# A token-embedding, gated-scan and ternary feed-forward kernel: the low-rank branch moved into row and column tiles of the matmul array

## What is computed

```
h = take(embed_table, x)                                   # [64, 256, 256]
h = h + minGRU(layernorm(h))     # f = sigmoid(x Wf'), i = sigmoid(x Wi'), g(x Wh')
                                 # state[t] = f*state[t-1] + i*g, started at 0.5
h = h + ffn(layernorm(h)):
    a = bitlinear(x, w_fc) + gate * (x @ v.T @ fast_b.T @ u.T)   # 256 -> 1024, and rank 16
    r = maximum(a, 0)
    return bitlinear(r * r, w_proj)                               # 1024 -> 256
```

## Time and profile before

| | before |
|---|---|
| median of 3 runs | 933.69 us (933.27 to 934.51) |
| time of the profiled execution | 933.25 us |
| its span, first to last instruction | 931.4 us |
| around the span (933.25 - 931.4) | 1.85 us |
| mean granted TensorE clock | 0.992 |
| busy: PE, DVE, ACT, POOL | 96%, 80%, 84%, 50% |

### The profile page before, as it was taken

How to read it: one execution, slowest core, us unless ns; L and a number is a source line. 1 busy time by engine, 2 the same in 40 slices (tenths; PEclk the granted TensorE clock), 3 DMA queues, 4 the chain that set the end, 5 groups by cost and what they waited for, 6 DMA issues and landing times.

```text
span 931.4 us, 17427 instructions
## 1 busy us (share of the span) xinstructions
PE 893.2 (96%) x5169; PEld 511.4 (55%) x5169; DVE 745.0 (80%) x1309; ACT 781.3 (84%) x1159; POOL 462.6 (50%) x457
## 2 busy tenths in 40 slices
PE   3889999999999999999999999999999999999976
PEld 2335555555555555555555555655555555555544
DVE  6799888878888878888887788888888888877663
ACT  4578998888898888889888889988888998888765
POOL 6545554556655455664545566554556555522110
PEclk9989999999999999999999999999999999999989
DMA  4223344342333333233333323323332332343220
GB/s 143 46 50 62 94 67 91 97 91 61 82 83 78 85 96 87 58 87 79 78 90 95 79 65 85 81 73 96 96 74 69 84 83 73 96 91 70 64 71 24
DMA packets 229579, 73.91 MB, mean 79 GB/s; under 512 B 204342, under 2 KB 224384, under 8 KB 229552
## 3 DMA queue, kind: packets, MB, share of 16 engines
q1 hardware_dynamic: 223408, 69.38, 31.3%
q0 software_dynamic: 6144, 4.21, 2.0%
HBM read 27.68 MB, written 24.64 MB: 56 GB/s over the span
## 4 chain that ended last, share of the span: by engine, by line
PE 91%; ACT 3%; DVE 2%; issue 2%; POOL 1%; DMA 1%; SPq 0%; ACTq 0%; POOLq 0%; DVEq 0%
PE bank L762 35%; PE y_ps L719 23%; PE bank L801 23%; PE bank L805 6%; PE bank L702 3%; PE turned L730 2%; ACT normed L476 1%; ACT relu L528 1%; ACT sq L541 1%; DMA w_raw<-wh 0%; POOL rows_raw L379 0%; DMA x_cols<-x_rows 0%; DVE stats L877 0%; POOL rstd L394 0%; DVE y_sb L1064 0%
## 5 line engine op out<-in xcount | busy, mean ns | idle before, releaser
L801 PE MATMUL bank<-x_cols,fc_t 128*128 128x512 f16 x1024 | 265.4, 382 | 0.0
L389 POOL TENSOR_SCALAR var_eps<-moments 128x4 f32<-128x4 f32 x64 | 59.7, 933 | 355.1 <-DVE moments L881 355.0
L762 PE MATMUL bank<-x_cols,w_hi 128*128 128x512 f16 x768 | 229.8, 381 | 4.6 <-ACT cand_lin L517 3.0
L762 PE MATMUL bank<-x_cols,w_lo 128*128 128x512 f16 x768 | 229.4, 380 | 0.0
L719 PE MATMUL y_ps<-proj_t,sq_hi 128*128 128x256 bf16 x1024 | 225.6, 273 | 2.1 <-DVE sq_lo L1056 2.0
L719 PE MATMUL y_ps<-proj_t,sq_lo 128*128 128x256 bf16 x1024 | 225.6, 273 | 0.0
L379 POOL DMA_INDIRECT rows_raw<-table,idx_now x128 | 161.3, 1260 | 60.2 <-issue 31.0
L528 ACT ACTIVATE relu<-bank,relu_scale 128x512 f32<-128x512 f32 x256 | 165.2, 688 | 13.0 <-PE bank L805 13.0
L801 PEld LDWEIGHTS bank<-x_cols,fc_t 128*128 128x128 bf16 x1024 | 100.9, 99 | 115.4 <-issue 3.2
L1056 DVE TENSOR_TENSOR sq_lo<-sq,sq_hi 128x1024 f16<-128x1024 f32 x128 | 150.4, 1214 | 15.0 <-ACT sq L541 15.0
L476 ACT ACTIVATE normed<-h,shift,rstd 128x256 f32<-128x256 f32 x256 | 132.9, 605 | 8.7 <-POOL shift L397 8.7
(11 more groups left out here) (129 smaller groups left out, 929.0 us busy)
## 6 DMA issues: line engine op xcount, KB each, us to landing
out<-out_sb SPq DMA_DIRECT2D x32, 512.0 KB, 2.9
spill<-hid_blocks SPq DMA_DIRECT2D x30, 256.0 KB
hid_rows<-spill SPq DMA_DIRECT2D x120, 64.0 KB
rows_raw<-table,idx_now POOLq DMA_INDIRECT x128, 2.8
x_cols<-x_rows SPq DMA_TRANSPOSE x124
sq<-w_fc SPq DMA_DIRECT2D x1, 1024.0 KB
pj_raw<-w_proj SPq DMA_DIRECT2D x1, 1024.0 KB
w_raw<-wf SPq DMA_DIRECT2D x1, 256.0 KB
```

The costliest lines, as they stand in the source:

```text
L762: ins = pe.matmul(bank[gate_bank[p]][:, :], w[:, k, q, :], x_part(0, par, part)[:, :, k, :], start=(k == 0 and w is w_hi and part == 0), s ...
L801: pe.matmul(dst[:, :], fc_t[:, f, k, :], x_part(1, 0, part)[:, :, k, :], start=(k == 0 and part == 0), stop=False)
```

## The change

The low-rank branch is done in other shapes, and the PSUM banks are given out by another rule. Line numbers in this section with an a (L730a) are of the changed kernel.

- `low_a` shrinks to 32 columns. `low_parts` (L730a) issues four matmuls of 32 output rows, one for each combination of input half and input part, into four column tiles of the array: rows 0-31, 32-63, 64-95 and 96-127 of `low_ps`, half of the PSUM tensor `turned`. They are four partial sums, not yet added.
- ScalarE copies them to float16 (`part_high`), VectorE takes the remainder (`part_low`), and `low_sums` (L740a, L741a) multiplies both by `spread`, a 0/1 matrix made at the start, which adds the partial sums and repeats the result over all 128 rows.
- ScalarE (`low_high`) and VectorE (`low_low`) split that result again, into `low_hi` and `low_lo`.
- `narrow` (L836a) replaces the eight matmuls L805 by sixteen that use 32 rows each: for four hidden blocks at a time, block i uses rows 32i to 32i+31, so four row tiles of the array, first with `low_hi`, then with `low_lo`.
- In a steady step blocks 0 and 1 are opened by `wide`, then `narrow(0, 2)` runs over blocks 0 to 3, which ends blocks 0 and 1 and opens 2 and 3, and `wide` ends those; then blocks 4 to 7 in the same way. `free(f)` is the wait for the block's bank.
- Bank of gate p: `(p + 2*par) % 4`; bank of block f: `(f + 2 + 2*par) % 4`.
- The four transposes of the scanned state go to the other half of `turned` (`turn_upper`).

```diff
-                for k in range(KD):
-                    for part in range(2):
-                        ins = pe.matmul(bank[0][:, :], low_a[:, k, :], x_part(1, 0, part)[:, :, k, :],
-                                        start=(k == 0 and part == 0), stop=(k == KD - 1 and part == 1))
-                ins.then_inc(low_done, 1)
+                for k in range(KD):
+                    for part in range(2):
+                        at = slice(BLOCK * (2 * k + part), BLOCK * (2 * k + part + 1))
+                        ins = pe.matmul(low_ps[at, :], low_a[:, k, :, :].rearrange("p a r -> p (a r)"),
+                                        x_part(1, 0, part)[:, :, k, :], start=True, stop=True)
+                ins.then_inc(part_done, 1)
+
+            def low_sums(m):
...
+                pe.wait_ge(part_hi_ready, m + 1)
+                pe.wait_ge(part_lo_ready, m + 1)
+                pe.matmul(low_ps, spread[:, :], part_hi[:, :], start=True, stop=False)
+                pe.matmul(low_ps, spread[:, :], part_lo[:, :], start=False, stop=True).then_inc(low_done, 1)
...
+                def free(f):
+
+                    if f > 3:
+                        pe.wait_ge(relu_ready, FC * m + f - 3)
...
+                def narrow(first_f, opened):
+
+                    for f in range(first_f + opened, first_f + 4):
+                        free(f)
+                    for part, ready in ((low_hi, low_hi_ready), (low_lo, low_lo_ready)):
+                        pe.wait_ge(ready, m + 1)
+                        for i in range(4):
+                            f, at = first_f + i, slice(BLOCK * i, BLOCK * (i + 1))
+                            ins = pe.matmul(fc_bank(f, par)[:, :], low_u[at, f * P:(f + 1) * P], part[at, :],
+                                            start=(part is low_hi and i >= opened),
+                                            stop=(part is low_lo and i < opened))
+                            if part is low_lo and i < opened:
+                                ins.then_inc(fc_done, 1)
...
+                    for p in range(3):
+                        gate(p)
...
+                        project(n - 2)
+                    gate(3)
+                    if steady:
+                        low_parts(n, m)
+                    gate(4)
+                    gate(5)
...
+                    if steady:
+                        low_sums(m)
...
+                wide(0, True)
+                wide(1, True)
+                if steady and front:
+                    narrow(0, 2)
+                    wide(2, False)
+                    wide(3, False)
+                else:
+                    low_sums(m)
+                    wide(2, True)
+                    wide(3, True)
+                    narrow(0, 4)
+                wide(4, True)
+                wide(5, True)
+                if front and not first:
+                    turn_upper(n)
+                narrow(4, 2)
+                wide(6, False)
...
+                wide(7, False)
```

On ScalarE and VectorE:

```diff
+            def part_high(m):
+
+                act.wait_ge(part_done, m + 1)
+                wait(act, low_done, m)
+                act.activation(part_hi[:, :], low_ps, ACT.Copy).then_inc(part_hi_ready, 1)
...
-                act.activation(low[:, :], bank[0][:, :], ACT.Copy).then_inc(low_hi_ready, 1)
+                act.activation(low_hi[:, :], low_ps, ACT.Copy).then_inc(low_hi_ready, 1)
...
+                part_high(m)
+                if front:
+                    evict(n, par, 1, 1, inp, ACT.Sigmoid)
+                    evict(n, par, 1, 2, cand_sig, ACT.Sigmoid)
+                    evict(n, par, 1, 3, cand_lin, ACT.Identity, 0.5)
                 low_high(m)
-                if front:
-                    evict(n, 1, 2, cand_sig, ACT.Sigmoid)
-                    evict(n, 1, 3, cand_lin, ACT.Identity, 0.5)
                 back(n)
...
-                low_half()
+                part_low()
                 if ahead:
                     x_low(0, n + 1)
                 if front:
                     candidate(1)
+                low_low()
+                if front:
                     weigh(1)
                     scan(1)
```

More of the change, by code:

```diff
@@ L97, in build @@
         hid_rows = sb("hid_rows", [P, TILES, P])
-        low = sb("low", [P, CHUNK], F16)
+        part_hi = sb("part_hi", [P, CHUNK], F16)
+        part_lo = sb("part_lo", [P, CHUNK], F16)
+        low_hi = sb("low_hi", [P, CHUNK], F16)
+        low_lo = sb("low_lo", [P, CHUNK], F16)
         relu = sb("relu", [P, FC // 2, 2, CHUNK])
@@ L598, in step @@
                     scale_fc(1)
-                    evict(1, 1, 2, cand_sig, ACT.Sigmoid)
-                    evict(1, 1, 3, cand_lin, ACT.Identity, 0.5)
+                    part_high(0)
+                    evict(1, par, 1, 2, cand_sig, ACT.Sigmoid)
+                    evict(1, par, 1, 3, cand_lin, ACT.Identity, 0.5)
                     low_high(0)
@@ L741, in step, with gate @@
                 steady = not isinstance(n, int) or n > 2
-                n_late = second or steady
+                def gate(p):
+                    e, g = divmod(p, 3)
+                    if p < 4:
+                        wait(pe, relu_ready, FC * (n - 2) + 5 + p)
+                        if first:
+                            pe.wait_ge(gate_taken, 8)
+                    else:
+                        pe.wait_ge(gate_taken, 8 * n + (4, 4 if start else 3)[p - 4])
+                    q = 2 * g + e
+                    for k in range(KD):
+                        for w in (w_hi, w_lo):
+                            for part in range(2):
+                                ins = pe.matmul(gate_bank(p, par)[:, :], w[:, k, q, :], x_part(0, par, part)[:, :, k, :],
+                                                start=(k == 0 and w is w_hi and part == 0),
+                                                stop=(k == KD - 1 and w is w_lo and part == 1))
+                    ins.then_inc(gate_done, 1)
@@ new lines, in free, with wide @@
+                def free(f):
+                    if f > 3:
+                        pe.wait_ge(relu_ready, FC * m + f - 3)
+                    elif front:
+                        pe.wait_ge(gate_taken, 8 * n + (2, 5, 6, 8)[f])
+                    else:
+                        pe.wait_ge(relu_ready, FC * (n - 2) + (7, 8, 5, 6)[f])
+                def wide(f, opens):
+                    if opens:
+                        free(f)
+                    if first:
+                        pe.wait_ge(fc_landed[f // 4], 16)
+                    for k in range(KD):
+                        for part in range(2):
+                            ins = pe.matmul(fc_bank(f, par)[:, :], fc_t[:, f, k, :], x_part(1, 0, part)[:, :, k, :],
+                                            start=(opens and k == 0 and part == 0),
+                                            stop=(not opens and k == KD - 1 and part == 1))
+                    if not opens:
+                        ins.then_inc(fc_done, 1)
@@ L1139, in residual, with part_low, low_low @@
                     measure(1, c, h1[:, at, :, :])
-                def low_half():
+                def part_low():
+                    dve.wait_ge(part_hi_ready, m + 1)
+                    wait(dve, low_done, m)
+                    dve.tensor_tensor(part_lo[:, :], low_ps, part_hi[:, :], ALU.subtract).then_inc(part_lo_ready, 1)
+                def low_low():
                     dve.wait_ge(low_hi_ready, m + 1)
-                    dve.tensor_tensor(low[64:P, :], bank[0][64:P, :], low[64:P, :], ALU.subtract)\
-                        .then_inc(low_ready, 1)
+                    wait(dve, fc_done, FC * m)
+                    dve.tensor_tensor(low_lo[:, :], low_ps, low_hi[:, :], ALU.subtract).then_inc(low_lo_ready, 1)
                 if start:
```

195 lines of the change are left out of this document (87 added, 108 removed).

## The result

The changed kernel takes **981.87 us** (median of 4 executions, 981.03 to 982.74). The kernel before, run beside it on the same chip, takes 933.61 us. The ratio is 1.0515, with a 95% interval of 1.0497 to 1.0534: slower by 48 us. The forecast was 966.0 in a range of 946 to 992: the sign and the mechanism came out, and a third of the loss (15.9 of 48.3 us) was missing.

What follows compares the result with a forecast made beforehand. PE was taken to bound the kernel, never waiting in a steady step. From 933.25 us, 29 steady steps of +0.90 (0.30 + 0.35 + 0.25) add 26.1, start and end 6.6: 966.0 us, range 946 to 992.

Steps and rivals of the forecast that it cites:

- PE's own work: Matmul slots and projection on PE: 7 slots added, 12 removed, so the step would shrink by 1.08 to 26.20 us.
- The wait for `low_lo`: After gate 5, PE waits some 0.5 us for DVE's `low_lo`, done 2.87 us after that gate's end.
- The wait for relu 3: Before `narrow(4, 2)`, PE waits another 0.9 us for ACT; relu 0 to relu 3's end takes 4.46.
- Distance s between tiles: Time between starts of neighbouring tiles: 0 to 0.098 us, middle 0.05 taken, 0.35 a step.
- Change of shape d: Switching between array shapes, three times a step: 0 to 0.163 us each, middle 0.08 taken, 0.25 in all.
- Transposed inputs: Needed 1.73 us earlier, before gate 4; landing 2.81 after issue, 16.15 against PE's 16.06 to 16.3: nearly limiting, costing nothing.
- the ring: Chain from one `narrow(4, 2)` to the next that sets a steady step: 27.58 against 27.28, +0.30 us before tile costs.
- a first wait for DMA `x_cols` longer than both others: Sign against the prediction: PE's wait for transposed inputs exceeding its waits for `low_lo` and for the relu.
- Start and end: Steps 1, 2 and the last lose 1.9, about 2 and 2.7 us, together 6.6.
- Serial tiles: Rival: tiles don't go side by side, each tiled matmul takes a slot; 2.6 us a step, total 1015 us; chance 0.12.
- "Faster": Rival: both waits total under 1.08 us, so PE never waits for relu 3; step 26.20, total 900 us; chance 0.05.

Runs made afterwards that it cites:

- kernel 4: Column tiles after gate 4, four relus ahead of two squares, and low copies first, all three against the changed kernel: 936.02 us, a step of 27.05.
- Experiment 2: Against the changed kernel, ScalarE does relu 0 to 3 first and the squares of blocks 0 and 1 behind them: 950.62 us.
- experiment 6: Against kernel 4, one more matmul of 32 rows in each steady step between gates 0 and 1, so two more shape changes: 947.51 us.
- Experiment 1: Against the changed kernel, column tiles moved behind gate 4 and `part_high` behind the eviction of gate 4's result: 968.1 us, a step of 27.99.
- kernel 10: Against kernel 4, start and end reordered, `part_high` ahead of `inp`, output copy right behind `low_low`: 926.31 us, ratio 0.9932.
- kernels 9: Against kernel 4, start and end reordered, `part_high` ahead of `inp`, output copy behind the scan: 926.57 us, ratio 0.994.

## Why the forecast was right in sign and short in size

- **PE's own work: right.** 87 slots and the projection were to take 26.20 us a step; kernel 4, with the waits gone, comes to 26.20 once the shape changes and the 0.2 are taken off.
- **The wait for `low_lo`: right.** From gate 5's end to the narrow group I had 2.87; it is 445.42 - 442.57 = 2.85. From there to relu 0 it is 0.55 (I took 0.48).
- **The wait for relu 3: right in mechanism and size.** From relu 0's start to relu 3's end 4.46 was summed from rows before; it is 4.45 (445.97 to 449.18 + 1.24). Experiment 2 shows that it is the costliest of the three. From relu 3's end PE needs 0.10 to start again (450.52 - 450.42), not 0.03.
- **Distance s between tiles: too high.** 0.05 was taken as the middle of 0 and 0.098, for want of a row; it is 0.005. Seven times in the ring: 0.03 us, not 0.35. The estimate of about 4 ns from the Trainium skill ("TensorE: Matmul & The Clock Gate", Part 3) agrees with this trace's 0.40 us for four tiles, and would have been the better price.
- **Change of shape d: right.** 0.08 taken, bounds 0 and 0.163; 0.10 to 0.11 measured, by the timeline and by experiment 6. The Trainium skill ("TensorEngine Tiling (Array Packing)", key properties) says that a change of tiling mode drains the engine; this case's traces agree that a change costs time, but do not show what happens in it.
- **Transposed inputs: the step that failed.** The prediction put it so: "it is nearly a second limit; it costs nothing here". With the measured s, d and the wait terms above, the ring of `low_lo` and relus closes at 27.58 + 0.03 (s) + 0.31 (d) + 0.07 (to relu 0) + 0.07 (start again) - 0.03 (the two waits above) = 28.03. Experiment 1, in which that ring stands alone, has 27.99. The change has 28.55: the 0.56 between them is the second limit. The term that was mis-sized is the landing. From `narrow(4, 2)` to relu 4, to `x_rows`' end and to the issue of the second transpose the shown step has 0.77, 11.21 and 1.43 us, where 0.70, 11.2 and 1.44 were taken. From that issue to the tiles it has 3.12, and the next step 3.95, where 2.81 was taken from the last step of the kernel before, one instance. That the forecast of 28.18 came near 28.55 is in part luck: 0.32 too much for s against 0.56 too little here. Of what was missing, 9.4 us lie in the steady steps (35.5 against 26.1) and 7.2 in start and end (13.8 against 6.6).

What the 0.56 is made of can be read in part. In 16 of the 28 steps the tiles start 3.10 to 3.20 us after the second transpose's issue. In ten others it is 3.5 to 4.0, and in all ten GpSimd's first gather of table rows is issued 1.3 us ahead of the second transpose, as at 462.63; where it comes 0.8 us behind, as at 436.41, the start is early. In the DMA engines' records 96 packets of the gathers fall between issue and tiles in the long case, and 8 to 32 in the short one. In experiment 2 no gather comes ahead, and 26 of 28 starts are early. So the gather probably delays the landing, but no run moves it by itself, and one late start (3.90, in step 30) has no gather near it. Why even the early ones take 3.1 and not 2.81 stays open.

- **The prediction's own signs.** It named as a sign of being wrong a first wait for DMA `x_cols` longer than both others. By the idle time of the weight loads that is so (33.5 against 32.1 and 14.3 us), by that of the matmuls not (18.6 against 24.2), nor by the mean losses (0.56 against 0.75). The sign was near to being met, and rightly pointed at the step that failed.
- **Start and end: too low.** 3.9 and 2.7 were summed; 9.1 and 4.7 were measured. The step written out for chunk 1 is the larger part: the projection of step 2 starts at 89.97 instead of 82.36, so 7.6 of the 9.1 are lost by then, against 1.9 forecast. The forecast let relu 0 run at about 65.9. But `low_high` comes behind the sums, at 65.20 after 5.19 us of idle time, and ScalarE's order has the normalising of chunk 2 between it and relu 0, which starts at 69.04. The other 1.4 us fall into step 2 (2 forecast). In kernel 10 the start is 2.3 us longer than before, and the end 1.2. Which of the moves gets how much back was not separated.

```profile
65.20 0.60 ACT L529 ACTIVATE low_hi<-turned 128x512 f16<-128x512 f32 x1 [5.19 <-PE turned L741]
65.69 2.06 ACT L493 ACTIVATE normed<-h,shift,rstd 128x256 f32<-128x256 f32 x4
69.04 1.26 ACT L552 ACTIVATE relu<-bank,relu_scale 128x512 f32<-128x512 f32 x2 [0.20 <-DVE relu_scale L1085]
```

- **Rivals.** Serial tiles are ruled out by the four starts within 0.02 us. "Faster" needed the two waits to fall under 1.08 us together; in the changed kernel they are 0.38 + 0.75 = 1.13, and the third comes on top, but kernels 9 and 10 are that case, brought about by moving other engines' work.

## What to carry to other kernels

Packing small matmuls into array tiles saves slots, but a group that serves four outputs needs all its operands and all four banks at once, so it delays the first output and asks early for the last bank: look at what its consumers run between them before counting the slots. Put the evictions that free banks ahead of work that nobody waits for, and price each entry to and exit from a group of tiles (here 0.10 to 0.11 us). A reader of a transfer that is moved until only tenths of a microsecond of slack are left should not be costed with one instance of the landing time: look at several, and at what else is on the DMA engines at that moment.

## What the hardware showed that I had not expected

Weight loads of different tiles overlap. The weight loads of the changed kernel around the narrow group whose matmuls start at 445.42, and around gate 4's first matmul at 439.10:

```profile
444.82 0.10 PEld L836 LDWEIGHTS bank<-low_hi,low_u 32*128 32x128 f16 x4 [0.42 <-issue]
445.41 0.10 PEld L836 LDWEIGHTS bank<-low_lo,low_u 32*128 32x128 f16 x4 [0.49 <-DVE low_lo L1233]
...
439.10 0.11 PEld L800 LDWEIGHTS bank<-x_cols,w_hi 128*128 128x128 f16 x2 [0.23 <-issue]
439.33 0.31 PEld L800 LDWEIGHTS bank<-x_cols,w_lo 128*128 128x128 f16 x2
```

Four loads take 0.10 us together, where one of 128 rows takes 98 ns. So the loads do not keep neighbours 98 ns apart, as my upper end for s had it. The third line bears on d: between matmuls of one shape the weights are loaded ahead (the load at 439.33 belongs to the pair of matmuls that starts at 439.55), but behind a group of tiles the first load begins only with its own matmul, at 439.10. The exposed load would be about the 0.10 us that a change of shape costs; whether it is that, or the emptying of the array, no run tells apart. The cost is the same for 128 x 32 column tiles and 32 x 128 row tiles, and for four tiles or a single one: 0.32 to 0.33 us to the next full matmul in all of these.
